# Token routing by scattered rows, values spread by transfers, and a rebuilt first attention, in a two-layer mixture-of-experts kernel

## The reference, cut to what matters

```python
# x: (2, 1024, 128); two layers; mod = silu(c) @ wmod gives shift, scale, gate for both halves of a layer
h = layernorm(x) * (1 + ca) + sa
x = x + ga * attn0(h)              # layer 0: RWKV-4; layer 1: RWKV-6, 16 heads of 8
h = layernorm(x) * (1 + cb) + sb
x = x + gb * ffn(h)                # both layers: 8 experts, hidden 512, top 2 of softmax

# attn0, per channel and step:
#   p = max(pp, u+k); e1 = exp(pp-p); e2 = exp(u+k-p); y = (e1*aa + e2*v) / (e1*bb + e2)
#   p2 = max(pp+w, k); aa, bb = exp(pp+w-p2)*aa + exp(k-p2)*v, exp(pp+w-p2)*bb + exp(k-p2); pp = p2
# attn1, per head: y_t = r_t . (S + u * k_t v_t^T); S = d_t * S + k_t v_t^T   (S is 8x8)
#   before it: token-shift mixes by low-rank products; after it: group norm, gate silu(g), W_o
# ffn: out = sum over the two chosen experts e of gate_e * (act(h @ W1[e] + b1[e]) @ W2[e] + b2[e])
#   layer 0: gelu, with biases; layer 1: silu, without
```

## Time and profile before

| | us |
|---|---|
| runs | 666.99, 672.38, 674.42 |
| profiled execution, its span | 673.3 |
| PE busy | 514.8 (76%) |
| DVE busy | 330.1 (49%) |
| POOL busy | 256.1 (38%) |
| ACT busy | 203.3 (30%) |
| first expert product (L824) | 124.6 |
| first projection of attention 1, batch a (L918) | 266.2 |
| first scan of attention 1, batch a | 314.7 |
| first expert product of group 3 | 462.8 |
| first expert product of group 4 | 585 |
| last expert product (L824) | 650.5 |

### The profile page before, as it was taken

One profiled execution on the slowest core, in us unless ns is written; L12 is line 12 of the kernel. 1 busy time (PEld: TensorE's weight loads), 2 busy tenths in 40 slices (PEclk: granted clock), 3 DMA queues, 4 the chain that ended last, 5 costly groups with the idle time before them and its releaser, 6 DMA issues. The chain is left out here.

```text
span 673.3 us, 7874 instructions
## 1 busy us (share of the span) xinstructions
PE 514.8 (76%) x2600; PEld 371.7 (55%) x2600; DVE 330.1 (49%) x624; ACT 203.3 (30%) x457; POOL 256.1 (38%) x238
## 2 busy tenths in 40 slices
PE   6952444787988789997788679997788996777763
PEld 5420224476977677346355544534454986767663
DVE  2799997533600015435986687534777546100000
ACT  2042510325535335345122013025111443033330
POOL 1062600762465643102644000306975223646440
PEclk9785665696998899976999777568989998689897
DMA  7000005255564655203100201402342543757623
GB/s 234 0 0 1 0 28 190 52 133 145 178 203 136 220 200 154 65 28 88 47 8 2 62 0 57 182 12 67 84 100 82 173 143 85 242 161 216 185 86 125
DMA packets 28744, 70.27 MB, mean 104 GB/s; under 512 B 5938, under 2 KB 10662, under 8 KB 28704
## 3 DMA queue, kind: packets, MB, share of 16 engines
q1 hardware_dynamic: 18656, 57.43, 27.1%
q0 software_dynamic: 5888, 10.25, 6.2%
q10 hardware_dynamic: 4160, 2.10, 1.1%
HBM read 62.40 MB, written 9.18 MB: 106 GB/s over the span
## 5 line engine op out<-in xcount | busy, mean ns | idle before, releaser
L437 POOL DMA_INDIRECT y_rows<-ys,dest x92 | 98.1, 1067 | 171.2 <-ACT ys L600 156.0
L430 POOL DMA_INDIRECT xg<-h_rows,source x92 | 93.0, 1010 | 152.2 <-DVE source L1266 108.3
L839 PE MATMUL PP<-w_ring,hid 128*128 128x128 f32 x736 | 109.3, 296 | 29.9 <-ACT hid L587 15.0
L839 PEld LDWEIGHTS PP<-w_ring,hid 128*128 128x128 f32 x736 | 95.4, 201 | 44.5 <-issue 22.9
L824 PE MATMUL PP<-xs,w_ring 128*128 128x128 f32 x736 | 100.3, 289 | 1.5 <-ACT xs L574 0.8
L824 PEld LDWEIGHTS PP<-xs,w_ring 128*128 128x128 f32 x736 | 96.3, 206 | 6.6 <-issue 5.7
L1275 DVE SCALAR_TENSOR_TENSOR x<-PP,gate,x 128x512 f32<-128x512 f32 x8 | 6.0, 750 | 163.6 <-PE PP L885 94.9
L600 ACT ACTIVATE ys<-PP,slot_gate 128x128 f32<-128x128 f32 x92 | 33.8, 370 | 128.7 <-PE PP L839 101.3
L587 ACT ACTIVATE hid<-PP,b1q 128x128 f32<-128x128 f32 x184 | 51.9, 379 | 52.1 <-PE PP L824 36.1
L463 POOL TENSOR_TENSOR arena<-arena 128x512 f32<-128x512 f32 x32 | 38.0, 1189 | 21.7 <-DVE arena L1322 19.4
L945 PE MATMUL PP<-arena,consts 128*128 128x512 f32 x64 | 35.5, 637 | 11.0 <-POOL arena L463 10.7
(11 more groups left out here) (193 smaller groups left out, 747.7 us busy)
## 6 DMA issues: line engine op xcount, KB each, us to landing
w_ring<-experts_dram SPq DMA_DIRECT2D x92, 512.0 KB
h_rows<-htok ACTq DMA_DIRECT2D x4, 512.0 KB
xg<-h_rows,source POOLq DMA_INDIRECT x92
y_rows<-ys,dest POOLq DMA_INDIRECT x92
x<-x_t_dram SPq DMA_DIRECT2D x4, 256.0 KB, 5.9
out_t_dram<-x SPq DMA_DIRECT2D x4, 256.0 KB, 3.7
H<-wmod_dram SPq DMA_DIRECT2D x1, 768.0 KB, 6.7
consts<-consts_dram SPq DMA_DIRECT2D x1, 704.0 KB, 7.5
```

The costliest lines, as they stand in the source:

```text
L430: pool.indirect_dma_start(xg[:, n % XG, :], None, h_rows[h], bass.IndirectOffsetOnAxis(source[:, h % 2, q:q + 1], 0)).then_inc(s_xg[n % XG ...
L437: pool.indirect_dma_start(y_rows[h], bass.IndirectOffsetOnAxis(dest[:, h % 2, q:q + 1], 0), ys[:, n % YR, :], None, bounds_check=TOPK * T ...
L839: last = pe.matmul(ps, hid[:, n % HID, c * P:(c + 1) * P], w_ring[:, n % WR, FH + c * P:FH + (c + 1) * P], start=(c == 0 and h >= NB), sto ...
```

## The change

The computation is the same, with the same four groups, the same 23 blocks each and the same 512 KB of weights per block. What differs:

- **Routing.** The one-hot matrices, the 128 products of L802 and the indices of slots are gone. DVE only writes each row's slot number (`row_of`). Token rows go from `htok` in SBUF straight to their slots in a DRAM array `xg_rows` by 16 indirect scatters a group ("puts", L489; one per 128 tokens and choice). That array is filled with zeros once at the start (SP, four transfers, 6 MB), since some slots stay empty. A block's rows then come by direct loads of four blocks each, issued by SP (L420, 24 in all, ring of 3).
- **Outputs.** ACT copies without a gate (ring of 6), SP stores each block in order to `y_rows` (L429, 92), and after a group's last store POOL fetches each token's two rows by 16 indirect gathers ("gets", L504). The gates are written on the diagonals of a 128x128 matrix for each 128 tokens and choice (`dg`, one 2048-wide DVE instruction, L1262), and the closing products take `dg` where they took the identity. The bias b2 enters there too, with the gates transposed; the 46 bias products of L836 are gone.
- **POOL** has only puts and gets left, in the order `p32 g32 p32 g32`: the puts of groups 1 and 2, the gets of 1 and 2, the puts of 3 and 4, the gets of 3 and 4.
- **Attention 0** uses the step's difference d = k - pp: two relu and two exp on ACT, two sigmoids for the current step, Ln and Exp for both batches' division; four fewer arguments, no POOL work.
- **Attention 1.** v is stored to DRAM (`v_rows`) and comes back spread over the partitions by one SP load for each step (L451, 8 of 512 KB for a, 16 of 256 KB for b, ring of 3). Batch a's recurrence is 1024 wide, 8 steps. The product with k, the scan and the product with r are all on DVE, one after the other.
- **Layer norm and group norm.** The mean is taken off by a product with (I - 1/128) or its head-wise counterpart; ACT squares and copies straight from the accumulator.
- **SP** now issues, in one merged order, weight loads (w), slot loads (l), stores of y (y), spreads (v) and results (o). The weight ring has 5 places.
- The order strings of all engines are new.

```diff
-XG, WR, YR, HID = 8, 6, 4, 2
+GROUPS = ((0, 0, (0, 1)), (0, 1, (0, 1)), (1, 0, (0, 1)), (1, 1, (0, 1)))
+UNIT = 4
+WR, XG, HID, YR, VS = 5, 3, 2, 6, 3
-"a4 b4 g15 s2 g5 s g s g2 s6 g s g3 s g s2 g3 s g s2 g2 s g2 s g s2 g3 s g s2 g2 s g s g s2 g s11 a4 "
...
+"w5 l5 w2 y2 w y w y w2 y2 w2 y2 l w2 y2 w2 y2 l2 w2 y2 l w2 y2 l w y w y w y w y l w y w y w y l w y w y w y w y w "
...
+"p32 g32 p32 g32",
...
-def rows_of_tokens(h):
-    for p in range(YR):
-        sp.wait_ge(s_sc[p], 16 * ((NQ * (h + 1) - 1 - p) // YR + 1))
-    if h:
-        sp.wait_ge(s_fin, BPB * h)
-    sp.dma_start(yt.rearrange("p k t n -> p (k t) n"),
-                 y_rows[h].rearrange("(a p) n -> p a n", p=P)).then_inc(s_yt, 16)
+def slots():
+    for g in range(NG):
+        for u in range(UNITS[g]):
+            m = U0[g] + u
+            qs = in_unit(g, u)
+            yield
+            if u == 0:
+                sp.wait_ge(s_put, 16 * TOPK * G0[g + 1])
+            if m >= XG:
+                gone = m - XG
+                og = max(k for k in range(NG) if U0[k] <= gone)
+                sp.wait_ge(s_xt, Q0[og] + in_unit(og, gone - U0[og])[-1] + 1)
+            sp.dma_start(xg[:, m % XG, 0:len(qs), :],
+                         xg_rows[g][qs[0] * P:(qs[-1] + 1) * P, :].rearrange("(q p) n -> p q n", p=P)).then_inc(s_xg[m % XG], 16)
+def rows():
+    for g in range(NG):
+        for q in range(NQ[g]):
+            n = Q0[g] + q
+            yield
+            sp.wait_ge(s_ys, n + 1)
+            sp.dma_start(y_rows[g][q * P:(q + 1) * P, :], ys[:, n % YR, :]).then_inc(s_yst[n % YR], 16)
+            sp.dma_start(blk(v_rows[b], i), blk(A1[b]["V"], i)).then_inc(s_vst[b], 16)
...
+                sp.dma_start(vs[m % VS][:, 0:width],
+                             heads[j][:, at0:at0 + width].unsqueeze(1).broadcast_to([P // HK, HK, width])).then_inc(s_vs[m % VS], 16)
-def gather(h, q):
-    n = NQ * h + q
-    if q == 0:
-        pool.wait_ge(s_idx, h + 1)
-        pool.wait_ge(s_hrow, 16 * (h + 1))
-    if n >= XG:
-        pool.wait_ge(s_xt, n - XG + 1)
-    pool.indirect_dma_start(xg[:, n % XG, :], None, h_rows[h],
-                            bass.IndirectOffsetOnAxis(source[:, h % 2, q:q + 1], 0)).then_inc(s_xg[n % XG], 16)
-def scatter(h, q):
-    n = NQ * h + q
-    pool.wait_ge(s_ys, n + 1)
-    pool.indirect_dma_start(y_rows[h], bass.IndirectOffsetOnAxis(dest[:, h % 2, q:q + 1], 0), ys[:, n % YR, :], None,
-                            bounds_check=TOPK * T - 1, oob_is_err=False).then_inc(s_sc[n % YR], 16)
-            pool.wait_ge(s_S, n + 1)
-            if n % SLOTS == 0:
-                pool.wait_ge(s_mx, BPB * len(JOBS) * (b + 1))
-            if n >= 3:
-                pool.wait_ge(s_yps, n - 2)
-            pool.tensor_tensor(prod[n % 3], blk(A1[b]["R"], i), S[n % 2][:, 0:BLK], ALU.mult).then_inc(s_prod, 1)
+                if t == 0 and k == 0:
+                    pool.wait_ge(s_spot, g + 1)
+                    pool.wait_ge(s_zeroed, 16 * NG)
+                if t % TPB == 0 and k == 0:
+                    pool.wait_ge(s_htok, B0[g] + t // TPB + 1)
+                pool.indirect_dma_start(xg_rows[g], bass.IndirectOffsetOnAxis(row_of[:, g, k, t:t + 1], 0),
+                                        htok[:, t, :], None, bounds_check=NQ[g] * P - 1,
+                                        oob_is_err=False).then_inc(s_put, 16)
+                if t == 0 and k == 0:
+                    for p in range(YR):
+                        pool.wait_ge(s_yst[p], 16 * ((Q0[g + 1] - 1 - p) // YR + 1))
+                    if g:
+                        pool.wait_ge(s_fin, B0[g])
+                pool.indirect_dma_start(yt[:, k, t, :], None, y_rows[g],
+                                        bass.IndirectOffsetOnAxis(row_of[:, g, k, t:t + 1], 0)).then_inc(s_got[t // TPB], 16)
-    act.activation(ys[:, n % YR, :], PP[:, 2 + n % 2, 0:P], ACT.Copy,
-                   scale=slot_gate[:, h % 2, q:q + 1]).then_inc(s_ys, 1)
+        act.activation(ys[:, n % YR, :], second_bank(n), ACT.Copy).then_inc(s_ys, 1)
-    for name, (count, value) in (("dE1", (s_arg, 1)), ("dE2", (s_argp, 1)), ("d2", (s_arg, 3)), ("d1", (s_argp, 2))):
-        yield
-        act.wait_ge(count[b], value)
-        table(*EXP)
-        act.activation(A[name], A[name], ACT.Exp).then_inc(s_exp[b], 1)
+    act.activation(A["E1"], A["D"], ACT.Relu, bias=wpos).then_inc(s_rel[b], 1)
+    act.activation(A["E2"], A["D"], ACT.Relu, bias=wneg, scale=-1.0).then_inc(s_rel[b], 1)
-    for k in range(2):
-        yield
-        pe.wait_ge(s_inrow, 2 * h + k + 1)
-        for n in range(NT):
-            i = NT * k + n
-            last = pe.matmul(rest[:, 0:2 * NQ], inrow[b][:, i, :], inblk[:, i].rearrange("p a q -> p (a q)"),
-                             start=(i == 0), stop=(i == TOPK * NT - 1))
-    last.then_inc(s_inv, 1)
-        pe.matmul(ps, b2q[:, h % 2, q:q + 1].broadcast_to([NE, P]), b2[:], start=True, stop=False)
-                last = pe.matmul(rest[:, n * P:(n + 1) * P], yt[:, r, 4 * k + n, :], ident,
-                                 start=(r == 0), stop=(r == TOPK - 1))
+            for r in range(TOPK):
+                last = pe.matmul(rest[:, n * P:(n + 1) * P], yt[:, r, t, :], dg[:, r, t, :],
+                                 start=(F == 1 and r == 0), stop=(r == TOPK - 1))
-        pe.matmul(side(0), sel[:, j, :], blk(v_lo, i), start=True, stop=False)
-        pe.matmul(side(0), sel[:, j, :], blk(v_hi, i), start=False, stop=True).then_inc(s_vb, 1)
-        link(dve.reciprocal(den[:, part], den[:, part]))
-    link(dve.tensor_tensor(inrow[b][:, 0:half], upto[:].unsqueeze(1).broadcast_to([P, half, P]),
-                           spot[:, 3, 0:half].unsqueeze(2).broadcast_to([P, half, P]), ALU.is_equal))
...
+    dve.tensor_copy(row_of[:, g, :, 0:nt], spot[:, :, 0:nt]).then_inc(s_spot, 1)
...
+    if g:
+        dve.wait_ge(s_fin, B0[g])
+    dve.tensor_tensor(dg[:, :, 0:nt], ident[:].unsqueeze(1).unsqueeze(1).broadcast_to([P, TOPK, nt, P]),
+                      gates[:, g % 2, :, 0:nt].unsqueeze(3).broadcast_to([P, TOPK, nt, P]), ALU.mult).then_inc(s_dg, 1)
-        dve.tensor_tensor(kv[n % 2], blk(A["K"], i), side(0), ALU.mult).then_inc(s_kv, 1)
+        dve.tensor_tensor(kv[:, 0:width], A["K"][:, span], vs[m % VS][:, 0:width], ALU.mult).then_inc(s_kv[b], 1)
...
+        link(dve.tensor_tensor_scan(S[:, 1:width + 1], A["dec"][:, span], kv[:, 0:width], start, ALU.mult, ALU.add))
...
+        link_prod(b, j, n, part, dve.tensor_tensor(prod[n % 2][:, 0:width], A["R"][:, span], S[:, 0:width], ALU.mult))
```

1691 lines of the change are left out of this document (859 added, 832 removed), and 26 rows, old and new, of the table ORDER.

## The result

The changed kernel took 641.48 us as the median of four runs (634.91 to 645.75), the kernel before 670.29 (four runs): a ratio of 0.961, 95% interval 0.949 to 0.973. I had said 620 (585 to 660). The direction and the range held, the gain is 29 us instead of 50.

A forecast was written before the change was run, and what follows sets the result against it. No engine was near full; stages with different limits set the end. From 673.3 us profiled, -6 - 19 - 10 + 0 - 22 - 7 + 13 = -51 gave 622, 621 as a median, stated as 620 (585 to 660).

The forecast's parts named there:

- Opening: Up to the first expert product: 124.6 to about 119 us (-6), bounds +8 and -15.
- Groups 1 and 2: First expert product to a's first projection: 142 to 122.5 us (-19), with 43 blocks at 2.6 us ahead of it.
- Pace: Time per expert block: 2.6 us taken, between bounds of 2.2 and today's 2.96 to 3.5.
- rival 2: Expert blocks go at the floor, 2.2 to 2.3 us each: 27 us less, 594 us; chance 0.14.
- The two floors: Least time of an expert block: 2.2 us by the transfers and 2.2 us by PE.
- rival 3: Expert blocks stay at 3.0 us, perhaps by the loop through ACT and PE: 33 us more, 655 us; chance 0.15.
- Projections of a: First projection of a to its first scan: 49 to 38.5 us (-10), bounds 0 and -14.
- Recurrence to group 3: Recurrence of a to group 3's first product: 148 to 148 us (0), bounds -25 and +25.
- rival 4: DVE holds up POOL's puts and gets, 3.2 us each instead of 2.0 and 1.25: 651 us; chance 0.12.
- Groups 3 and 4: Group 3 to group 4: 123 to 100 us (-22); group 4: 68 to 61 us (-7).
- Tail: After the last expert product: 20.3 to 33 us (+13), of which 16 gets take 20 us, nothing hidden.
- Rival 5: SP's one strict queue becomes the bound, with stores holding up weight loads: 59 us more, 681 us; chance 0.07.

The follow-up runs named there:

- stores_from_act: The changed kernel with the 92 stores of block outputs issued by ScalarE, right behind the copy, instead of by SP: 639.47 us, ratio 0.954.
- one_in_flight: The changed kernel with each put of group 2 and each get of group 1 issued only when the one before has landed: 668.69 us, ratio 0.999.

## Why the prediction was right in sign and too high in gain

- **Opening.** 121.1 instead of 119. DVE's busy time there fell by 22 us (98.7 to 76.6), where I had 25 to 30; right within its bounds.
- **Groups 1 and 2: the step that failed.** I wrote that the gets of group 1 "run under group 2's blocks and cost nothing", and did not price the puts of group 2 beside group 1's blocks at all. I had read in the earlier trace rows what one indirect transfer takes on POOL, about 1 us, and took the work as hidden since POOL has nothing else to do. The runs showed 29.5 us for 28 such transfers, 1.05 us each, of which 18 to 21 come back when they are broken up (123.9 and 121.0 us against 141.6, forecast 122.5). The blocks themselves went faster than I had put them: without the two runs the stage is 112.1 us, 10 less than forecast. The miss of +19 is these two together.
- **What the trace of before could have told.** It has such a stop too. From 139.0 to 154.1 us POOL issues 12 indirect transfers 1.3 us apart, no product with W1 runs from 147.6 to 162.8, and ScalarE has the same waits without a name:

```profile
149.04 0.37 ACT L600 ACTIVATE ys<-PP,slot_gate 128x128 f32<-128x128 f32 x1 [6.08 <-remote]
156.12 2.17 ACT L587 ACTIVATE hid<-PP,b1q 128x128 f32<-128x128 f32 x8 [6.71 <-remote]
```

  I had read the 24.6 us of L600 as scatters that hold the ring of `ys`. But L587 and L591, which write `hid` and don't touch that ring, wait another 24.7 us for "remote"; together it is as much as in the changed kernel (50 and 54 us on ScalarE). So the price of such runs probably stood in the 142 us of this stage already, and the change kept it. No run of the kernel before tested that.
- **Pace.** I took 2.6 us a block; undisturbed it is 2.3 to 2.4, near what rival 2 had. The two floors were equal in my sum; with half the weights the pace stays, so that of the transfers doesn't bind here. The stage mean was 3.0, rival 3's number, but not for rival 3's reason alone: it named the loop through ACT and PE, and the runs show the indirect transfers.
- **Projections of a.** 41.6 for 38.5; TensorE is busy 38.0 of them. The 3 us were not looked into.
- **Recurrence to group 3.** 135.2 instead of 148. From the first scan to the first put it is 102.9 us, where I had 111; the puts took 24.6, not 32; from there to the first product 7.7, not 5. That I added the puts in series was wrong as well: with 14 of the 16 left out this stage is 3 us shorter. The rows of the puts, and of DVE beside them:

```profile
416.92 2.29 DVE L1262 TENSOR_TENSOR dg<-ident,gates_sb 128x2048 f32<-128x2048 f32 x1
418.04 2.01 POOL L489 DMA_INDIRECT xg_rows<-htok,row_of  x1 [0.30 <-issue]
...
419.91 1.23 DVE L1337 TENSOR_TENSOR_SCAN arena<-arena 128x512 f32<-128x512 f32 x1
420.36 1.56 POOL L489 DMA_INDIRECT xg_rows<-htok,row_of  x1 [0.30 <-issue]
...
423.82 0.97 POOL L489 DMA_INDIRECT xg_rows<-htok,row_of  x1 [0.30 <-issue]
```

  Nine of the 16 puts take 1.27 to 2.01 us, the other seven 0.97. Each of the nine starts while a DVE instruction runs, and its extra time is what is left of that instruction, less 0.10 to 0.19 us: the put at 418.04 takes 1.04 us more than 0.97, and the instruction ahead of it ends at 419.21, 1.17 us later. A DVE instruction that starts after the put costs it nothing. The two of the earlier trace rows fit too: 0.84 and 0.96 us more, with 0.97 and 1.10 us left. So rival 4's 3.2 us for each is out; the 16 puts lose 4.4 us in all. The spread loads came in time: DVE has no gap of note there, where I had put 11 us. The rule of the Trainium skill that I cited for rival 4 (page "SBUF — State Buffer", section "Who interferes with whom"), that whichever issues first keeps the shared pair for its whole instruction, agrees with these rows, in amount too; what I had wrong was to charge each transfer a whole scan of 2.28 us instead of the rest of one.
- **Groups 3 and 4.** 94.4 for 100 and 66.1 for 61. Both hold a stop. In the first, the way to group 4's first put took 54.7 us where I had 72, and from there to the first product 39.6 where I had 28: the first slot load is issued 12.6 us behind the last put (527.0 and 514.4), behind the last weight loads and stores of group 3 in SP's order, of which none went out between 506.5 and 517.7. That the two nearly cancel is luck. Group 4, from first to last L870, takes 64.1 us; without its stop 53 to 55.
- **Tail.** 33.1 for 33. The rows in the chain of waits:

```profile
600.54 1.52 DMA y_rows<-ys
...
623.09 2.46 DMA yt<-y_rows,row_of
625.68 3.77 PE PP L911 x16
629.47 0.75 DVE x L1271
```

  Between the first and the second of these stand 16 gets, most of them 1.25 us apart. Direct loads in their place make the tail 12.7 us shorter; I had expected 13 to 15.
- **Rival 5.** It didn't come about (stores_from_act), but one_in_flight shows a like mechanism at 668.7 us: not stores but a slot load that waits for a late put holds the weight loads behind it.

The errors, +2, +19, +3, -13, -6 and +5, give the 11 us between the forecast of 622 and the profile. That +19 and -13 have opposite signs is luck: no mechanism joins them. The profiled execution (633.1) was itself 8 us under the first median.

## What to carry to other kernels

Work that is hidden on an idle engine still shares something with the others: price a run of indirect transfers by what it does beside the main loop, not by its own line. Where such a run must go beside the blocks, issue a few (four here) and wait for their landing before the next few, or use direct loads where the rows allow it. And when a rare wait is put into a queue that all transfers share, look at what stands behind it; one late put held the weights for 32 us.
